# A four-layer vision tower: its second layer and the last layer's attention each in one block, the scan's start and the third layer's loop in another order

## What is computed

```python
h = _L0_tok_ref(x, L0_tok_W, L0_tok_b)
h = h + L0_attn(ln(h))        # softmax attention, one head
h = h + L0_ffn(ln(h))         # 16 experts, top 2, and a shared one
h = h + L1_attn(ln(h))        # linear attention, no softmax
h = h + L1_ffn(ln(h))         # router bits; 12 heads; fc1, gelu, fc2; low rank
h = h + L2_attn(ln(h))        # selective scan over 192 x 16 states
h = h + L2_ffn(ln(h))         # 128 experts, top 6, and a shared one
h = h + L3_attn(ln(h))        # 12 heads, only the largest scores of a row
h = h + L3_ffn(ln(h))         # 16 experts, top 3 and a common one
```

```python
h = x + bits[:, :, 0:1] * (softmax(q k^T / 4) v @ wo.T + bo)
out = h + bits[:, :, 1:2] * (gelu(ln(h) @ fc1.T + b1) @ fc2.T + b2)
out = out + (low-rank product chosen by the two bits)
```

## Time and profile before

| | |
|---|---|
| three executions | 944.35, 944.51, 948.4 us, median 944.51 |
| the profiled execution | 950.86 us, its span 949.0 |
| mean granted TensorE clock | 0.907 of full |
| TensorE busy | 840.1 us, 89% of the span |
| VectorE, ScalarE, GpSimd busy | 396.7, 303.6, 291.6 us |
| matmuls, and all instructions | 6257, 18563 |

### The profile page before, as it was taken

One profiled execution on the slowest core, in us unless ns is written; L12 is line 12 of the kernel. 1 busy time (PEld: TensorE's weight loads), 2 busy tenths in 40 slices (PEclk: granted clock), 3 DMA queues, 4 the chain that ended last, 5 costly groups with the idle time before them and its releaser, 6 DMA issues. The chain is left out here.

```text
span 949.0 us, 18563 instructions
## 1 busy us (share of the span) xinstructions
PE 840.1 (89%) x6257; PEld 682.3 (72%) x6257; DVE 396.7 (42%) x1184; ACT 303.6 (32%) x633; POOL 291.6 (31%) x321
## 2 busy tenths in 40 slices
PE   8996999899989869999979999999789959889891
PEld 6775988565666449997548999999455847688881
DVE  1353222323451347886572222222152883444443
ACT  2430222215343066663301222222224223334340
POOL 0013555100020137771123444444110000247772
PEclk9987999988888979999779999999899778789995
DMA  9616989200000142210165898989813300658885
GB/s 358 255 43 211 304 259 301 69 1 1 1 2 0 38 167 77 73 40 1 40 218 160 314 299 303 323 279 300 240 44 121 111 2 18 184 166 263 255 266 167
DMA packets 56443, 148.84 MB, mean 157 GB/s; under 512 B 7952, under 2 KB 18944, under 8 KB 55872
## 3 DMA queue, kind: packets, MB, share of 16 engines
q1 hardware_dynamic: 47296, 125.10, 39.4%
q0 software_dynamic: 9088, 22.98, 8.7%
HBM read 134.58 MB, written 13.47 MB: 156 GB/s over the span
## 5 line engine op out<-in xcount | busy, mean ns | idle before, releaser
L1554 POOL DMA_INDIRECT L_xr<-x_rows_L,L_rows_in x92 | 93.9, 1021 | 40.3 <-issue 33.6
L2357 DVE TENSOR_TENSOR L_act<-L_hid,bank 116x512 f32<-116x512 f32 (+1 forms) x56 | 35.9, 640 | 160.8 <-ACT L_hid L2326 90.3
L2246 POOL DMA_INDIRECT y_rows_L<-L_yb,L_rows_out x56 | 55.8, 996 | 106.6 <-ACT L_yb L2332 97.3
L2326 ACT ACTIVATE L_hid<-bank 116x512 f32<-116x512 f32 (+1 forms) x56 | 31.3, 559 | 167.3 <-PE bank L2296 157.3
L2290 PE MATMUL bank<-L_xtb,L_w 128*116 128x128 f32 (+1 forms) x464 | 57.8, 278 | 0.1
L2290 PEld LDWEIGHTS bank<-L_xtb,L_w 128*116 128x116 f32 (+1 forms) x464 | 55.0, 187 | 0.7 <-issue 0.6
L2306 PE MATMUL bank<-L_w,L_act 116*128 116x192 f32 (+1 forms) x232 | 46.1, 340 | 2.7 <-ACT L_yb L2332 2.7
L1461 POOL TENSOR_TENSOR ssm_w_low<-ssm_wbc,ssm_w_high 128x512 fp32r<-128x512 f32 x24 | 31.4, 1310 | 42.5 <-ACT ssm_w_high L1419 42.5
L1620 POOL TENSOR_TENSOR L_s_up<-L_s_hid,L_s_up 116x288 f32<-116x288 f32 (+1 forms) x10 | 7.9, 794 | 114.6 <-ACT L_s_up L1614 114.6
L2290 PE MATMUL bank<-L_xtb,L_more 128*116 128x128 f32 (+1 forms) x352 | 42.7, 273 | 0.0
L2306 PEld LDWEIGHTS bank<-L_w,L_act 116*128 116x128 f32 (+1 forms) x232 | 36.8, 189 | 6.7 <-ACT L_yb L2332 2.9
(11 more groups left out here) (460 smaller groups left out, 1888.1 us busy)
## 6 DMA issues: line engine op xcount, KB each, us to landing
L_w<-in_L2w SPq DMA_DIRECT2D x20, 696.0 KB
L_more<-in_L2w SPq DMA_DIRECT2D x20, 696.0 KB
L_w<-in_L2w SPq DMA_DIRECT2D x20, 384.0 KB
L_more<-in_L2w SPq DMA_DIRECT2D x20, 384.0 KB
L_w<-in_L0w SPq DMA_DIRECT2D x12, 576.0 KB
L_more<-in_L0w SPq DMA_DIRECT2D x12, 576.0 KB
ssm_wbc<-in_wBC SPq DMA_DIRECT2D x24, 256.0 KB
L_w<-in_L3w SPq DMA_DIRECT2D x16, 384.0 KB
```

The lines of the kernel that those rows point to most:

```text
L1554: pool.indirect_dma_start(self.xr[j][:, :], None, self.x_rows[:, :], bass.IndirectOffsetOnAxis(ap=at, axis=0))\
L2246: pool.indirect_dma_start(X.y_rows[:, :], bass.IndirectOffsetOnAxis(ap=rows_out[h][:, j:j + 1], axis=0), y[s + j][:, :], None).then_inc(st ...
L2326: act.activation(hid[j][:, :, :], cols(gate_bank[j % 2][0:N, 0:C * R], C), ACT.Silu).then_inc(acted, 1)
L2357: dve.tensor_tensor(act_out[j][:, :, :], hid[j][:, :, :], cols(up_bank[j % 2][0:N, 0:C * R], C), ALU.mult)\
```

## The change

1. **The second layer is one block.** `head_attention` and `feed_forward` no longer open blocks of their own; they get the one that the linear attention and the projections run in. What the barrier assured is waited for by semaphores: `head_projections` returns `ready`, which TensorE and GpSimd call before the scores and the memset, and `head_attention` returns `att_in`, on which the output projection waits by halves. The masks of GpSimd wait until the norm behind the residual is done. To make room, tensors of stages that no longer have a block of their own are laid into others: q, k, v and the product of the linear attention into `qk` and `wide`, the router's and the norm's into `scores`, the activation of fc1 into `probs_t`.
2. **The last layer's attention is one block**, with an output projection of its own, by halves of the tokens; `linear`, `residual` and `biased` are gone.
3. **The scan's start.** ScalarE does its part of the norm before the first two casts of weights. Delta is made for plane 1 first, with `Ln` and the sum in two halves. The first tile's product of decay less one and x is one instruction of VectorE. The cast for tile 2 stands after the first decay, the low part for tile 3 before GpSimd's loop. Two wakes stand before TensorE's loop over tiles.
4. **The third layer's loop** has five inner passes in a group instead of four (and four groups instead of five).
5. **The closing wake** of the first and third layer's tails is one instead of two.

The core of the diff:

```diff
-    "L2": dict(experts=128, top=6, pairs=6, cap=192, width=464, chunks=4, group=4, between=(6, 0, 2, 2), by_tile=(0, 2)),
+    "L2": dict(experts=128, top=6, pairs=6, cap=192, width=464, chunks=4, group=5, between=(6, 0, 2, 2), by_tile=(0, 2)),
...
+    @block.gpsimd
+    def _(pool):
+        ready(pool, True)
+        pool.memset(padded[:, :, SEQ:TALL], 0.0).then_inc(cleared, 1)
+
+    @block.tensor
+    def _(pe):
+        for g in range(BATCHES):
+            ready(pe, g > 0)
...
+    def ready(pe, banks):
+
+        pe.wait_ge(qk_in, 8)
+        pe.wait_ge(spread_q, 6)
+        if router:
+            pe.wait_ge(router.chosen, 4)
+        if banks:
+            pe.wait_ge(v_second_in, VU)
...
+        for s in range(2):
+            pe.wait_ge(att_in, 4 * s + 4)
...
+        pool.wait_ge(norm.normalized, 2)
+        link(pool.tensor_scalar(inv[:, :, :], bits[:, :, :], -1.0, 1.0, ALU.mult, ALU.add))
...
             project(0, 1, c_made)
             pe.wait_ge(relu_made, 2)
+            wake(T, T.bank[2 * SUM_AT], 2)
             for t in range(n_tiles):
...
+            norm.act(act)
             split_high(0)
             split_high(1)
-            norm.act(act)
-            for m in range(2):
-                act.wait_ge(pre_made, m + 1)
+            for i, m in enumerate((1, 0)):
+                act.wait_ge(pre_made, i + 1)
...
             act.wait_ge(soft, 1)
-            act.activation(mag[:, :, :], mag[:, :, :], ACT.Ln, bias=1.0).then_inc(soft, 1)
-            split_high(2)
+            for m in (1, 0):
+                act.activation(mag[:, m, :], mag[:, m, :], ACT.Ln, bias=1.0).then_inc(soft, 1)
+            T.load_table(ACT.Exp)
             for t in range(n_tiles):
...
             for t in range(n_tiles):
                 d, st = decay[t % NB], state[t % NB]
-                dve.wait_ge(grown_made, t + 1)
+                if t == 0:
+                    dve.wait_ge(decayed, 1)
+                    dve.scalar_tensor_tensor(grown[0][:, :], d[:, :], -1.0, xs[:, of(0), :], ALU.add, ALU.mult).then_inc(first_grown, 1)
+                    dve.wait_ge(first_grown, 1)
+                else:
+                    dve.wait_ge(grown_made, t)
...
-        wake(T, T.bank[7], BRIDGE)
+        wake(T, T.bank[7], BRIDGE // 2)
```

More of the change, by code:

```diff
@@ L620, in wide_layer, with head_attention @@
     return h_in
-def head_attention(T, name, qk, wide, v, vb, att, sparse, also=None):
+def head_attention(T, ctx, block, name, ready, qk, wide, v, vb, att, sparse, also=None, space=None):
     nc = T.nc
@@ L830 @@
+    return att_in
 class SecondWeights:
@@ new lines, in _ @@
+        for s in range(2):
+            pe.wait_ge(down_in, 2 * s + 2)
+            for m in range(2):
+                for k, part in enumerate((d01, d2)):
+                    mm = pe.matmul(up_bank[s][m][:, 0:HALF], up[k][:, 128 * m:128 * m + 128], part[:, at(s)], start=(k == 0), stop=(k == 1))
+                mm.then_inc(up_made, 1)
+        wake(T, T.bank[0], BRIDGE // 2)
+    @block.scalar
+    def _(act):
+        norm.act(act)
+        for s in range(2):
+            for m in range(FC):
+                act.wait_ge(fc1_made, FC * s + m + 1)
+                act.activation(mid[:, m, at(s)], fc1_bank[s][m][:, 0:HALF], ACT.Gelu, bias=p["fc1b"][:, m:m + 1]).then_inc(mid_in, 1)
```

724 lines of the change are left out of this document (321 added, 403 removed).

## The result

The changed kernel takes 918.14 us in the median of 4 executions (916.22 to 918.42), the kernel before 944.43 (4 executions): ratio 0.9708, interval 0.9679 to 0.9737. Timed twice more, each time with both kernels on one chip, it came to 918.45 against 943.66 and 920.0 against 943.66, ratio 0.9741 both times (0.9709 to 0.9772 and 0.9707 to 0.9775). So the change gains 24 to 28 us. The forecast was 20.3 us; the first ratio puts the time at 916.9 (0.9708 x 944.5), 0.6 under the range, the later two at 920.0, inside it.

What follows compares the result with a forecast made beforehand. TensorE was taken as the bound wherever it has work; only its standing still and half clock could be won. Terms summed to 20.3 us, 944.51 - 20.3 = 924.2; range 921 to 927, or 917.5 to 931.5 with A and most of B.

Steps and rivals of the forecast that it cites:

- the seams: Block boundaries before scores and output projection: TensorE's idle time goes, 1.2 and 1.0 us (second layer), 1.3 and 1.0 (last).
- the masks: Second layer: GpSimd's selection masks held back until after the second norm, so residual adds lose their slow form, 2.0 us.
- the norm without its clock part: Scan's layer norm: ScalarE squares before casting weights; gain 4.1 us in all, with some 1.2 of 4.25 being clock.
- the first tile: Scan: Ln to first product falls from 5.98 to 4.41 us, a gain of 1.6 (0.3 to 1.9).
- the empty passes: Third layer's loop end: three empty passes on TensorE go with five inner passes in a group, 3.5 us.
- the 64 matmuls: Shared expert after the third layer's loop: full clock takes them from 16.86 to 14.7 us, gain 2.1 (none to 2.1).
- Rival B: More clock: TensorE stays at full clock through scores, second norm and first scan tiles; gain 26, 918.5 us; chance 0.14.
- The load of the table: ScalarE before the second layer's scores: load takes 1.28 us without a drain, so the 1.2 us gain there stands.
- The fetched rows: Third layer's tail: fetched results move up about 1 us, landing just in time or half a microsecond late.
- rival A: Stalls go but time is given back through clock, late row fetch and first-tile contention; gain 12.6 at worst, 929.5; chance 0.20.
- C: Slower: halved closing wakes let the clock fall at the second and last layers' starts; 42 us more, net 966; chance 0.03.
- D: Little happens: waits hidden before now show and fetched results set the loop's end; about 941 us; chance 0.05.

Runs made afterwards that it cites:

- the masks' run: Changed kernel, but GpSimd's four selection masks begin when the attention's last batch is in, as before the change: 930.12 us, ratio 0.9780, on another chip.

## Why the prediction was nearly right, and where it failed

**The idle time was right as a sum.** The forecast's terms of standing still are the seams (4.5), the masks (2.0), the norm without its clock part (2.9), the first tile (1.6) and the empty passes (3.5), 14.5; the two wakes in the scan fill 1.9 more. That is 16.4, and the profiles say 15.3. In the table's last column the four seams gave 3.3 of their 4.5, since waits for the softmax took the place of some of the idle time, the masks 1.4 of 2.0, the loop 4.2 instead of 3.5. The single steps: column sums to projection 6.59 (forecast 6.7), Ln to product 4.25 (4.41), the new VectorE operation 0.76, the lower bound (0.82 taken), residual adds 0.46, idle time at the loop's end 1.57 (1.6), the 64 matmuls 14.73 (14.7), seams gone. For the first tile the lower bound of the term is a gain of 2.0, not 1.9. The slow side of the first tile's bounds never came up, because GpSimd was idle until 330.85, when the operation of 330.29 was over half done. The upper bound itself, 0.76 times 2.7, was read wrongly: the masks' run shows an add that waits until the mask under way is done, not one that runs 2.7 times slower.

**The step that failed is the clock, which the sum put at nothing outside three places.** The forecast gave it 2.1 (the 64 matmuls) + 0.5 (the scan's tiles) + 1.2 (the scan's norm) = 3.8 us; the wakes cancel, 2.0 out and 1.9 in. TensorE's busy time fell by 11.1, so the term was mis-sized by 7.3. In its three places it was about right, 1.7, 0.6 and 0.9 (the 0.6 mostly without the wakes that it was given for). The missing 8 us are in the stages where the sum has no clock at all: the second layer's linear attention 1.9, its second norm and projections 1.1, the attention 1.7, output projection and norm 1.0, fc1 and after 0.7, the last layer's projections 1.7 and attention 1.1, and 0.4 each in the first layer and in the third layer's loop, less 1.1 and 0.9 given back in the third layer's routing and the last layer's experts.

Some of this belongs to the change: the scores (1.3, in 13 of 14 profiles with one block), and 1.0 with the masks' place (TensorE's busy time is 0.2 longer with early masks up to fc1, and 0.8 behind it). The linear attention's 1.9 do not: nothing was edited there, and it took 24.34 us in one of four profiles before and in all three after, but 25.5 to 28.8 in seven of the variants of the changed kernel. For the other stages no run tells change from chance. Rival B, which said 26 us, was right in size, partly by luck: it named the scores, the norm behind the output projection (1.0) and the first tiles (little), and its reason, that without the seam TensorE stays at full clock through the scores, is not what the profiles show; the clock falls in the scores in every one, in most only for a shorter time.

**Seams** cost more than their idle time, 3.5 to 4.7 us for two and 2.5 to 3.5 for the last layer's two, against 2.2 and 2.3; the second layer's 1.3 beyond it repeats in every profile with the seam. The prediction read the branch's idle time and took it for the whole price. **The load of the table** cost 1.30, with no drain: the Trainium skill's 2.66 (ScalarE: Activation LUTs, What ACT_TABLE_LOAD costs) would have kept the first score copy until about 245.8 (an estimate, 243.11 and that figure), and it stands at 244.52. ScalarE does come late by more than before, 2.48 us after the scores' start instead of 1.7, and four copies follow each other without a wait; TensorE finished its scores earlier all the same. **The fetched rows**, rival A's bound, were issued at 652.79 and landed 8.6 and 13.3 us after their issues, the last at about 666.5; VectorE took the first half at 663.39 and the second at 666.84, 0.3 later, so nobody waited, and the tail is 30.0 us. Rival A did not happen, by two errors that cancelled: the fetch did not move up by 1 us against the loop's last matmul (6.92 us behind it before, 6.82 now), and the second half is wanted 3.44 us after the first, not 1.95, since two more additions stand between (693.86 and 697.30 before). **C**, the slower case, did not happen: both windows of the layers' starts are at 0.93 or more. Its test without any closing wake is one profile. **D**, little gain, did not happen.

The error in method: the forecast rested on one profile of the kernel before, which at 950.86 us was 6.4 above the median. Four of them show which stage lengths repeat (attention 22.07 to 22.10) and which are drawn anew (linear attention 24.34 to 27.47). Such a stage can't be a term; it is a width, and a range that ended at 917.5 was too narrow on this side. The two later ratios put the time inside it, at 920.0; the 0.6 us by which the first lies outside are less than the spread of the changed kernel's own executions, 916.2 to 924.3.

## What to carry to other kernels

Divide the gain into TensorE's idle time and its busy time at the same count of matmuls: the first answers to semaphores, barriers and order and can be summed from one profile; the second is the clock, and wants several profiles or an interval of several microseconds. Where a block boundary stands in front of many small matmuls, count more than the branch's idle time (1.3 us more here, for a reason not found). After idle time is cut, look for the gaps of one or two microseconds ahead of stretches at half clock, put a wake there that ends with the gap, and time it: two of them in the second layer's norm gained about 4 us here, nine more another 5.5, and those in the scan next to nothing.

## What the runs showed of the hardware

VectorE's add with two operands in SBUF takes 0.46 us alone. Beside GpSimd's masks it ended 0.30 to 0.33 us after the mask that it met, whether that one had one operand or two, and so took 0.51 to 1.24. VectorE's operations between the adds, whose first operand is in PSUM, took 0.50 to 0.52 with the masks and without. The Trainium skill (GPSIMD Engine Reference, Specifications) names the shared interfaces and VectorE's two operands, and the trace agrees; that the add waits for the end of GpSimd's operation is what these rows add. And an unchanged program has stages whose length falls on a few values, 6.59 or 8.79, 58.6 or 60.3, 24.34 to 27.47, with the granted clock beside each.
